# Result added on GpSimd, a bracket made in two parts, search values copied ahead of a drain, row-maximum scalars made on ScalarE

## The reference

```
Rf = S / rowsum(S);  Rb = S / colsum(S)          # S: 3327 x 3327, given, plus the identity
for s in range(2):
    Q, K = Xa @ W1, Xa @ W3
    logits = Q @ W2 @ K.T                        # 3327 x 3327
    keep the largest logits of each row until their softmax sums to 0.9
    A  = softmax(kept logits)
    Xf = Rf @ Xf;  Xb = Rb @ Xb;  Xa = A @ Xa
    Z += Xf @ U1[s] + Xb @ U2[s] + Xa @ U3[s]
Y = X + Z
out = x + (Y - mean(Y)) / sqrt(var(Y) + 1e-5) * gamma + beta
```

## Time and profile before

| | us |
|---|---|
| median of 3 runs | 2001.48 (1999.96 to 2001.77) |
| the profiled execution, its own time | 1999.62 |
| its span | 1997.6 |
| before step 0 | 0 to 307 |
| step 0, 26 tiles | 307 to 1065 |
| step 1, 26 tiles | 1065 to 1964 |
| last moments, finish, stores | 1964 to 1997.6 |
| busy in the span: PE, DVE, ACT, POOL | 1777, 1634, 1365, 605 |

### The profile page before, as it was taken

One profiled execution on the slowest core, in us unless ns is written; L12 is line 12 of the kernel. 1 busy time (PEld: TensorE's weight loads), 2 busy tenths in 40 slices (PEclk: granted clock), 3 DMA queues, 4 the chain that ended last, 5 costly groups with the idle time before them and its releaser, 6 DMA issues.

```text
span 1997.6 us, 37487 instructions
## 1 busy us (share of the span) xinstructions
PE 1777.0 (89%) x11660; PEld 1312.2 (66%) x11660; DVE 1634.1 (82%) x3964; ACT 1364.9 (68%) x2201; POOL 605.1 (30%) x1056
## 2 busy tenths in 40 slices
PE   4999964899999999993976699999999999999997
PEld 3888832677777777773763466666666676767665
DVE  5444467899999999998864899999999999999987
ACT  5222266888888888983835568686868686777752
POOL 4000131244444444441341132324242323232330
PEclk9999976899999999997988899999999999999998
DMA  6999721454444444442433010101010101010122
GB/s 170 196 202 203 195 100 56 97 117 117 112 105 116 106 111 114 110 108 56 112 77 125 22 42 21 42 21 42 21 42 21 42 21 42 21 41 22 38 91 72
DMA packets 235345, 168.26 MB, mean 84 GB/s; under 512 B 188451, under 2 KB 220577, under 8 KB 235168
## 3 DMA queue, kind: packets, MB, share of 16 engines
q1 hardware_dynamic: 221264, 117.44, 21.6%
q0 software_dynamic: 3744, 22.14, 7.2%
q10 hardware_dynamic: 10288, 28.12, 4.2%
HBM read 107.99 MB, written 37.49 MB: 73 GB/s over the span
## 4 chain that ended last, share of the span: by engine, by line
issue 35%; DVE 21%; PE 19%; POOLq 9%; DVEq 7%; POOL 4%; DMA 2%; ACT 2%; ACTq 0%
DVE probs_t L1588 7%; DVE stats L1595 5%; POOLq L720 5%; PE lg L1165 2%; DMA probs_t<-row_scalars 2%; PE bank L1096 2%; PE bank L1095 2%; PE bank L1079 2%; PE lg L1096 2%; PE lg L1095 2%; PE bank L1200 2%; DVEq L1783 1%; DVE sorted_e L1614 1%; PE bank L1052 1%; DVEq L1612 1%
## 5 line engine op out<-in xcount | busy, mean ns | idle before, releaser
L1188 PE MATMUL bank<-both,s_tile 128*128 128x512 f16 x1352 | 302.4, 381 | 16.9 <-issue 16.9
L1257 PE MATMUL bank<-xcur,probs_t 128*128 128x256 f32 x1352 | 296.1, 379 | 0.0
L1165 PE MATMUL lg<-k_t,q_tile 64*128 64x512 f32 (+1 forms) x820 | 191.6, 568 | 96.1 <-DVE expo L1485 89.1
L1257 PEld LDWEIGHTS bank<-xcur,probs_t 128*128 128x128 f32 x1352 | 255.0, 190 | 33.6
L1188 PEld LDWEIGHTS bank<-both,s_tile 128*128 128x128 bf16 x1352 | 132.8, 98 | 166.7 <-issue 20.0
L1485 DVE TENSOR_SCALAR_CACHE_REDUCE expo<-lg 128x1024 f32 (+1 forms) x208 | 206.8, 1023 | 43.1 <-PE lg L1165 27.4
L660 POOL TENSOR_TENSOR window<-window,probs_t 128x832 f16<-128x832 f32 x104 | 215.2, 2069 | 81.1 <-ACT probs_t L937 68.6
L1165 PEld LDWEIGHTS lg<-k_t,q_tile 64*128 64x128 f32 x820 | 69.3, 192 | 178.6 <-DVE expo L1485 123.1
L868 ACT ACTIVATE expo<-expo,below_max 128x3327 f32<-128x3327 f32 x52 | 159.4, 3065 | 24.7 <-DVE below_max L1493 23.7
L699 POOL TENSOR_TENSOR aims<-found 128x2 f32<-128x2 f32 x26 | 5.1, 195 | 555.6 <-ACT found L903 555.6
L1588 DVE SCALAR_TENSOR_TENSOR probs_t<-expo,mine 128x1664 f32 (+3 forms) x54 | 156.4, 2896 | 8.4 <-issue 8.0
(11 more groups left out here) (303 smaller groups left out, 3628.6 us busy)
## 6 DMA issues: line engine op xcount, KB each, us to landing
s_tile<-s_scratch SPq DMA_DIRECT2D x28, 832.0 KB, 4.5
expo<-in_adj POOLq DMA_DIRECT2D x25, 831.8 KB, 9.7
s_tile<-s_scratch ACTq DMA_DIRECT2D x24, 832.0 KB, 4.5
s_scratch<-s_tile SPq DMA_DIRECT2D x14, 832.0 KB, 10.1
s_scratch<-probs_t SPq DMA_DIRECT2D x6, 832.0 KB, 9.3
s_scratch<-window SPq DMA_DIRECT2D x6, 832.0 KB, 9.6
q_tile<-q_scratch SPq DMA_DIRECT2D x104, 32.0 KB, 2.1
xa_scratch<-ht ACTq DMA_DIRECT2D x26, 128.0 KB, 2.2
```

Of the source, the lines that this page charges most:

```text
L1165: last = T.matmul(lg[c % 2][:, h * CHUNK:h * CHUNK + w], q_tile[b][DA * h:DA * (h + 1), :], k_all[DA * h:DA * (h + 1), s, c0:c0 + w], star ...
L1188: last = T.matmul(s_ps[:, 0:width], s_tile[b][:, k, :], moving, start=(k == 0 and part == 0), stop=(k == NT - 1 and part == 1))
L1257: last = T.matmul(kept_ps[1][:, 0:D], probs_t[:, k * P:(k + 1) * P], xcur[:, k, :], start=(k == 0), stop=(k == NT - 1))
```

## The change

1. **Row-maximum scalars on ScalarE, both steps.** DVE stops after the row maximum, now kept for each buffer in `tops`. L1493 is gone; ACT makes the two biases in `exponentials` by two Identity activations of one column, with a drain, ahead of the exponential.
2. **Search values copied ahead of a drain, both steps.** DVE's order was chunks, drain, maximum, drain, L1493, copy into `mine`, drain. It is now chunks, copy into `mine`, drain, maximum, drain. So the maximum of the next tile stands behind the copy, and behind the wait for `cut_ready` or `lead_ready`.
3. **Bracket in two parts, step 1.** `first_bracket` starts at a new semaphore, `first_counted` (ACT's first count), and does the part of the first point; only the second point and the interpolation wait for `expo_ready[1]`.
4. **Stored result added on GpSimd, step 1.** For tiles 0 to 24, POOL adds `y_in` to ACT's copy of the products (`add_result`). PE's product with the identity stays for the last tile alone. SP loads the next `y_in` when the add is done, and the sum, mean and squares of tile t are made in ACT's step t + 1, between `refine` and the wait for `fb_turned`; in the last step behind the last L997.

The diff, with less context and without one entry of a table of semaphores:

```diff
--- before
+++ after
@@ -173,6 +173,7 @@
...
         offsets = row_scalars[:, 0:2]
+        tops = sb("tops", [P, 2])
         centre = row_scalars[:, 2:3]
...
@@ -346,7 +347,9 @@
...
         lead_ready = sem("lead_ready")
+        first_counted = sem("first_counted")
         x_added = sem("x_added")
+        y_added = sem("y_added")
         lo_ready = [sem(f"lo_ready_{n}") for n in range(2)]
...
@@ -571,7 +575,7 @@
...
                     load_s(t + 1, m + b, 1 - b)
-                sp.wait_ge(y_done[1], t + 1)
+                sp.wait_ge(y_added, t + 1)
                 sp.dma_start(y_in[:, :], dram_tile(y_dram, tile_of(m, b))).then_inc(y_loaded[1], DMA)
...
@@ -694,30 +698,33 @@
...
             def first_bracket(t, m, b):
-                pool.wait_ge(expo_ready[1], t + 1)
-                ends, whole = lead[:, b, 8:12], found[:, b, 4:5]
-                G.tensor_tensor(aims[:, :], found[:, b, 1:4:2], found[:, b, 6:7].broadcast_to([P, 2]), ALU.add)
-                G.tensor_copy(lead[:, b, 4:7], found[:, b, 4:7])
-                G.tensor_copy(scalar_points[:, 0:4:2], found[:, b, 0:4:2])
-                G.tensor_scalar(ends, ends_t[:, :], whole, None, ALU.mult)
-                G.tensor_scalar(span[:, :], found[:, b, 0:4:2], AIM[1] + GUARD, None, ALU.mult)
-                pool.drain()
-                G.tensor_tensor(ends, ends, ends_c[:, :], ALU.add)
-                G.tensor_tensor(aims[:, :], aims[:, :], span[:, :], ALU.add)
-                pool.drain()
-                G.tensor_scalar(scalar_points[:, 1:4:2], aims[:, :], -1.0, None, ALU.mult)
-                pool.drain()
-                for r in range(2):
+                ends, whole, minus_slack = lead[:, b, 8:12], found[:, b, 4:5], aims[:, 0:1]
+
+                def offer(r):
+                    place = scalar_points[:, 2 * r:2 * r + 1]
+                    G.tensor_tensor(span[:, 0:1], minus_slack, found[:, b, 2 * r + 1:2 * r + 2], ALU.subtract)
+                    G.tensor_copy(place, found[:, b, 2 * r:2 * r + 1])
+                    pool.drain()
+                    G.tensor_scalar(scalar_points[:, 2 * r + 1:2 * r + 2], found[:, b, 2 * r:2 * r + 1], -(AIM[1] + GUARD), span[:, 0:1], ALU.mult, ALU.add)
+                    pool.drain()
                     G.tensor_scalar(picked[:, r, 0:4], sides[:, :], scalar_points[:, 2 * r + 1:2 * r + 2], 0.0, ALU.mult, ALU.is_gt)
                     G.tensor_scalar(left_out[:, r, :], sides[:, :], scalar_points[:, 2 * r + 1:2 * r + 2], 0.0, ALU.mult, ALU.is_le)
-                pool.drain()
-                for r in range(2):
+                    pool.drain()
                     G.tensor_tensor(pairs(picked[:, r, 4:8]), pairs(picked[:, r, 0:4]), twice(scalar_points[:, 2 * r:2 * r + 2]), ALU.mult)
-                for r in range(2):
                     G.tensor_tensor(ends, ends, left_out[:, r, :], ALU.mult)
...
                     pool.drain()
+
+                pool.wait_ge(first_counted, t + 1)
+                G.tensor_tensor(minus_slack, ends_t[:, 0:1], found[:, b, 6:7], ALU.subtract)
+                G.tensor_copy(lead[:, b, 4:7], found[:, b, 4:7])
+                G.tensor_scalar(ends, ends_t[:, :], whole, None, ALU.mult)
+                pool.drain()
+                G.tensor_tensor(ends, ends, ends_c[:, :], ALU.add)
+                offer(0)
+                pool.wait_ge(expo_ready[1], t + 1)
+                offer(1)
                 G.tensor_tensor(span[:, :], lead[:, b, 10:12], lead[:, b, 8:10], ALU.subtract)
...
@@ -730,6 +737,12 @@
...
                 G.tensor_scalar(lead[:, b, 12:16], sides[:, :], lead[:, b, 3:4], None, ALU.mult).then_inc(lead_ready, 1)
+            def add_result(t, m, b):
+                y = tile3(y_all, tile_of(m, b))
+                pool.wait_ge(y_out[1], t + 2)
+                pool.wait_ge(y_loaded[1], DMA * (t + 1))
+                G.tensor_tensor(y, y, y_in[:, :], ALU.add).then_inc(y_added, 1)
+
             def centre_result(t, m, b):
...
@@ -740,11 +753,15 @@
...
             pool.wait_ge(gamma_in, DMA * 2)
-            with pool.Fori(0, NT // 2 - 1) as i:
-                for b in range(2):
-                    first_bracket(i * 2 + b + 2, i + 1, b)
-                    centre_result(i * 2 + b, i, b)
-            centre_result(NT - 2, NT // 2 - 1, 0)
+
+            def results(t, m, b):
+                if not (isinstance(t, int) and t >= NT - 2):
+                    first_bracket(t + 2, m + 1, b)
+                if not (isinstance(t, int) and t == 0):
+                    centre_result(t - 1, m - 1 + b, 1 - b)
+                if not is_last(t):
+                    add_result(t, m, b)
+            skewed_loop(pool, results)
 
...
@@ -865,6 +882,9 @@
...
                     act.wait_ge(logits_copied[s], t + 1)
+                    for j in range(2):
+                        A.activation(below_max_all[:, b, j:j + 1], tops[:, b:b + 1], ACT.Identity, scale=-1.0, bias=offsets[:, j:j + 1])
+                    act.drain()
                     A.activation(expo[b][:, 0:N], expo[b][:, 0:N], ACT.Exp, bias=neg_max[b],
...
@@ -901,8 +921,9 @@
...
                     last = A.activation(minus_under[b][r], neg_count[:, :], ACT.Identity, scale=tried[b][r], bias=lack[:, :])
+                    if s == 1:
+                        last.then_inc((first_counted, expo_ready[1])[r], 1)
                     if s == 1 and r == 1:
-                        last.then_inc(expo_ready[1], 1)
                         return
...
@@ -989,14 +1010,28 @@
...
 
+                def result_moments(m, b):
+                    y, column = tile3(y_all, tile_of(m, b)), bass.ds(tile_of(m, b), 1)
+                    act.drain()
+                    A.activation(mean[:, column], y_sum[:, :], ACT.Copy, scale=-1.0 / D)
+                    act.drain()
+                    A.activation(turned[:, 0:D], y, ACT.Square, bias=mean[:, column], accum_out=var[:, column]).then_inc(y_moments, 1)
+
+                def added_result(t, m, b):
+                    A.activation(turned[:, 0:D], tile3(y_all, tile_of(m, b)), ACT.Copy, accum_out=y_sum[:, :])
+                    result_moments(m, b)
+
                 def step(t, m, b):
                     more = not (isinstance(t, int) and t >= NT - 2)
+                    before = None if isinstance(t, int) and t == 0 else (t - 1, m - 1 + b, 1 - b)
 
...
                     if is_last(t):
+                        act.wait_ge(y_added, t + 1)
+                        added_result(*before)
                         act.wait_ge(var_ready, 1)
...
@@ -1005,8 +1040,12 @@
...
                     A.activation(ht[b][:, :], pv_ps[:, 0:D], ACT.Copy, scale=kept_inv[b]).then_inc(xa_ready[1], 1)
+                    if before is not None and not is_last(t):
+                        act.wait_ge(y_added, t + 1)
                     if more:
                         refine(b, 1)
+                    if before is not None and not is_last(t):
+                        added_result(*before)
                     act.drain()
...
@@ -1015,12 +1054,12 @@
...
                     act.wait_ge(y_done[1], t + 2)
-                    y, column = tile3(y_all, tile_of(m, b)), bass.ds(tile_of(m, b), 1)
-                    A.activation(y, pv_ps[:, 0:D], ACT.Copy, accum_out=y_sum[:, :]).then_inc(y_out[1], 1)
-                    act.drain()
-                    A.activation(mean[:, column], y_sum[:, :], ACT.Copy, scale=-1.0 / D)
-                    act.drain()
-                    A.activation(turned[:, 0:D], y, ACT.Square, bias=mean[:, column], accum_out=var[:, column]).then_inc(y_moments, 1)
+                    y = tile3(y_all, tile_of(m, b))
+                    if is_last(t):
+                        A.activation(y, pv_ps[:, 0:D], ACT.Copy, accum_out=y_sum[:, :]).then_inc(y_out[1], 1)
+                        result_moments(m, b)
+                    else:
+                        A.activation(y, pv_ps[:, 0:D], ACT.Copy).then_inc(y_out[1], 1)
                 for t in range(2):
...
@@ -1030,7 +1069,7 @@
...
                 else:
-                    tiles_loop(act, step)
+                    skewed_loop(act, step)
             act.wait_ge(var_ready, 2)
...
@@ -1265,9 +1304,10 @@
...
                     pe.wait_ge(x_t_ready[1], t + 1)
-                    pe.wait_ge(y_loaded[1], DMA * (t + 1))
-                    T.matmul(pv_ps[:, 0:D], ident[:, :], y_in[:, :], start=True, stop=False)
-                    products(t, True)
+                    if is_last(t):
+                        pe.wait_ge(y_loaded[1], DMA * (t + 1))
+                        T.matmul(pv_ps[:, 0:D], ident[:, :], y_in[:, :], start=True, stop=False)
+                    products(t, is_last(t))
 
...
@@ -1458,11 +1498,6 @@
...
 
-            def below_max(b):
-                if isinstance(b, int):
-                    return below_max_all[:, b, :]
-                return below_max_all[:, bass.ds(b, 1), :].rearrange("p a n -> p (a n)")
-
             def of_two(buf, b):
...
@@ -1485,13 +1520,10 @@
...
```

(18 more changed lines are left out.)

1 line of the change is left out of this document (added).

## The result

The changed kernel takes 2004.8 us (median of 20 runs, 1999.45 to 2006.78), the kernel before 2000.83 (median of 20 runs, 1999.6 to 2003.34). The ratio is 1.002, with a 95% interval of 1.0014 to 1.0026. The forecast was 2005, in a range of 1994 to 2014. The total was right, and it was right by luck: two errors cancel. Step 0 lost 16 us more than I said, and the steady part of step 1, where I had forecast a loss of 1, gained 13.

What follows compares the result with a forecast made beforehand. ScalarE was taken to bound step 0, VectorE step 1. Terms +0.4 − 2.3 + 1.1 + 5.0 = +4.2 us gave 2003.8 on the profiled execution, 2005.7 on the median; forecast 2005, range 1994 to 2014.

Steps and rivals of the forecast that it cites:

- Tail, +5.0: End of kernel: VectorE waits 7.4 us for tile 24's moments, delaying the last store; +2.5 to +5.7, taken as +5.0.
- Start of step 1, −2.3: Start of step 1: bracket in two parts shortens VectorE's wait, −2.6 us, plus 0.3 for ScalarE's Identities.
- Table load: Start of step 0: ScalarE's table load, earlier inside a wait, now stands behind the Identities on the path; +1.28 us.
- the rival: Step 0: COPY caught until GpSimd's piece ends, 3.43 us after L937 starts; period 26.84, about +9; chances 0.17 and 0.08.
- I take that case, with a margin of only 0.2: Step 0: VectorE's COPY is asked for 0.2 us ahead of GpSimd's first piece, so is not held; period 26.38, +0.41.
- The two prices of the sum: Step 0, per tile: 0.41 us for the Identities on ScalarE, another 0.46 if COPY is held behind GpSimd's piece.
- First and last tiles of step 0: Step 0, where VectorE is the bound: together −4.7 us by tile 4, and −1.9 each for tiles 22 and 23.
- Steady step 1: Steady tiles of step 1: +0.05 us per tile over 23 tiles, +1.1; without GpSimd's hold of VectorE, −8.7.
- The hold: Steady step 1: GpSimd's 0.58 us power L731 holds VectorE's two-input L1661, turning −0.38 per tile into +0.15 in tiles hit.
- the gain: Steady step 1: VectorE saves 0.38 us per tile without L1493 and its drain, and with COPY in a drain's shadow.
- the free L1661: Steady step 1: L1661 passes without GpSimd's hold; −8.7 us in place of +1.1, 1995; no or half hold 0.25.
- the forecast case: Steps 0 and 1 together: COPY early and L1661 held; 2002 to 2008 us, chance 0.42.

## Why the prediction was right, and where it was not

- **Tail, +5.0: right.** Measured +5.6, by the mechanism named: the wait (6.31 for 7.4 forecast), then the last store behind the big ones. The upper bound of 5.7 was the right one.
- **Start of step 1, −2.3: right.** Measured −2.5, and VectorE's wait is 2.0 shorter. The stage itself is known to about 1 us only; the wait is 4.56 to 4.59 in all eight variants that leave this code as it is, and 8.00 with the bracket in one part.
- **Table load: right**, 1.28 in the open.
- **Step 0: the rival came true, not the forecast.** The step that failed is "I take that case, with a margin of only 0.2". The copy was caught: it ended with GpSimd's piece at A + 3.46 and L888 came at A + 4.36, a period of 26.83; the rival had A + 3.43, A + 4.4 and 26.84. What was wrong in my choice is the premise that ScalarE's lateness would move A back until TensorE's wait was used up. TensorE still waits 1.24. VectorE is put back in every tile by a second hold, which I had not looked for: GpSimd's L655 on the scan, 0.87 to 1.02 long in place of 0.29. That this hold decides between the two states is read from the rows and was not tested by itself. I had also used the steady 22.49 of ScalarE's work for tile 0, where it is less: kept_inv(1) ended at 370.69 and L958 started 0.41 behind it. The two prices of the sum were near: 0.41 forecast for the Identities, 0.36 measured; 0.46 for the hold, 0.50 measured.
- **First and last tiles of step 0: wrong by 3.0 and 3.9.** Only the first interval gained as said (25.40 for 25.5). The second and that from tile 22 to 23 gained 0.9 and 1.0 in place of 1.9. From the second on the copy was held as everywhere else, so the gains that I had for tiles 2 to 4 and 22 to 25 were those of the state that did not come.
- **Steady step 1: wrong, by 13.9 us.** Two terms failed. The hold: L1661 was to be held by a power of one column. It started 0.06 to 0.19 ahead of it in the steady tiles, but that margin is not the reason; placed inside it, it is not held either (0.14 long). I had carried the price of the pieces of 832 columns over to a power of one column. And the gain: 0.38 per tile was 0.54, because the drain between the maximum and the pass over the row is gone too, which I had left in. 23 × 0.54 is 12.4, near the 12.8 measured.
- **The sum.** With the rival's step 0 and the free L1661 the prediction had 2004, at a chance of 0.08. That case came, and the range held it, but the forecast case at 0.42 did not: 2005 was met by +14.7 and −12.8 where +7.0 and +1.1 stood. Even the 2004 was met by errors that cancel: it had −8.7 for step 1 where −12.8 came, and about 7 us too little for step 0. A period of step 0 that did not grow was named as what would show the prediction wrong, and it grew, by twice the forecast; that of step 1, 33.4, was named for the case without a hold (33.30 measured).

## What to carry to other kernels

Compare a forecast with the trace stage by stage, not by its total: here a total within 0.2 us of the measured one hid errors of 16 and 14 us. Moving small work off one engine pays only where the engine that takes it is not the bound of that stage: the same edit cost 0.86 us per tile in step 0, where ScalarE is the bound (0.36 of it for the moved work itself), and brought 0.54 in step 1, where VectorE is. And when an order of small operations is changed, look at which of them can be held by a neighbour and who waits behind it; a maximum that was not held was put behind a copy that was.
